# A one-hot product padded from 64 to 128 rows, and the last tile's end moved from GpSimd to VectorE and ScalarE

## The reference, cut to what matters

```python
h = _ln(x, pw_g[pathway_ids], pw_b[pathway_ids])
h = _ln(h, cp_g[compartment_ids], cp_b[compartment_ids])
t = _ln(x, tm_g[time_steps], tm_b[time_steps])
m, n, r = (x + _mlp_ln(state, ...)[:, None, :] for each of three states)
s = _ln(x, ms_g[scale_type], ms_b[scale_type])
cat = concatenate([w[0]*h, w[1]*t, w[2]*m, w[3]*n, w[4]*r, w[5]*s])
x = x + _ln(silu(cat @ int_W1 + int_b1) @ int_W2 + int_b2, int_g, int_be)
```

## Time and profile before

| | |
|---|---|
| time, 3 runs | 1055.29, 1057.88, 1057.75 us; median 1057.75 us |
| profiled execution: its own time, its span | 1056.21 us, 1054.3 us |
| PE busy, share of the span | 996.6 us, 95% |
| DVE, ACT, POOL busy | 664.7 us (63%), 486.1 us (46%), 703.6 us (67%) |
| mean granted clock of TensorE | 0.985 |
| chain that ended last, by engine | PE 76%, DVE 7%, issue 6%, POOL 5%, ACT 3% |

### The profile page before, as it was taken

How to read it: one execution, slowest core, us unless ns; L and a number is a source line. 1 busy time by engine, 2 the same in 40 slices (tenths; PEclk the granted TensorE clock), 3 DMA queues, 4 the chain that set the end, 5 groups by cost and what they waited for, 6 DMA issues and landing times.

```text
span 1054.3 us, 18130 instructions
## 1 busy us (share of the span) xinstructions
PE 996.6 (95%) x6546; PEld 780.5 (74%) x6546; DVE 664.7 (63%) x1210; ACT 486.1 (46%) x763; POOL 703.6 (67%) x635
## 2 busy tenths in 40 slices
PE   6989999999999796999999999999999999999993
PEld 3566777767777475888888887888888888888882
DVE  5677777678768767657557558556556556555441
ACT  2678768775767534334334335324324324323321
POOL 4556665667665348758768768767767767777852
PEclk9989999999999998999999999999999999999997
DMA  9634653544322554232232234233223233132310
GB/s 265 220 118 136 210 212 142 197 167 138 131 88 62 154 178 138 70 104 92 75 115 97 73 111 142 72 95 120 69 92 124 65 101 120 62 108 77 103 42 20
DMA packets 56156, 124.04 MB, mean 118 GB/s; under 512 B 7827, under 2 KB 10005, under 8 KB 55044
## 3 DMA queue, kind: packets, MB, share of 16 engines
q1 hardware_dynamic: 44292, 80.94, 22.9%
q0 software_dynamic: 11776, 41.95, 12.9%
HBM read 104.91 MB, written 17.95 MB: 117 GB/s over the span
## 4 chain that ended last, share of the span: by engine, by line
PE 76%; DVE 7%; issue 6%; POOL 5%; ACT 3%; DMA 1%; SPq 0%; POOLq 0%; DVEq 0%; ACTq 0%
PE ps L597 39%; PE ps_y L604 7%; PE ps_k L669 6%; PE ps_o L604 5%; PE tp L609 5%; PE ps_v L658 2%; PE tp L897 2%; PE ps_s L645 1%; PE ps L976 1%; PE ps_u L690 1%; POOL kb L1669 1%; POOL e L1663 1%; PE ps_z L885 1%; DVE xl L1313 1%; ACT k_diag L993 1%
## 5 line engine op out<-in xcount | busy, mean ns | idle before, releaser
L1715 POOL TENSOR_TENSOR rstd<-var_eps,half 128x1 f32<-128x1 f32 x96 | 54.7, 570 | 118.5 <-DVE var_eps L1510 117.7
L1647 POOL TENSOR_TENSOR om<-om,bc 128x512 f32<-128x512 f32 x32 | 48.1, 1504 | 82.6 <-DVE om L1319 82.6
L1184 ACT ACTIVATE g_out<-ps 128x512 f32<-128x512 f32 x32 | 19.1, 598 | 178.0 <-PE ps L976 178.0
L993 ACT ACTIVATE at_diag<-at 32x512 f32<-32x512 f32 x128 | 80.2, 626 | 7.8 <-DVE at L1293 6.7
L1516 DVE TENSOR_SCALAR shift_n<-mean_var,rstd 128x1 f32<-128x1 f32 x96 | 20.5, 214 | 97.1 <-POOL rstd L1715 95.1
L993 ACT ACTIVATE k_diag<-kt 32x512 f32<-32x512 f32 x128 | 80.1, 625 | 1.1
L1496 DVE TENSOR_TENSOR t_lo<-tp,t_hi 128x512 fp32r<-128x512 f32 x64 | 43.8, 684 | 31.3 <-ACT t_hi L1121 31.3
L1125 ACT ACTIVATE h<-h,shift_n,rstd 128x512 f32<-128x512 f32 x32 | 26.1, 816 | 80.1 <-DVE shift_n L1516 80.1
L1659 POOL TENSOR_SCALAR xb<-xb,bias_o 128x512 f32<-128x512 f32 x32 | 52.2, 1633 | 11.3 <-DMA xb<-in_x_wide 11.2
L1663 POOL TENSOR_TENSOR e<-e,rinv 128x512 f32<-128x512 f32 x32 | 33.6, 1051 | 36.4 <-DVE rinv L1280 36.4
L669 PE MATMUL ps_k<-wk_hi,xh 128*128 128x512 f32 x128 | 55.8, 436 | 0.2 <-DVE xl L1313 0.2
(11 more groups left out here) (286 smaller groups left out, 3240.6 us busy)
## 6 DMA issues: line engine op xcount, KB each, us to landing
raw<-in_dec_w SPq DMA_DIRECT2D x30, 512.0 KB, 6.1
x_in<-in_x_turned SPq DMA_DIRECT2D x32, 256.0 KB, 5.3
xb<-in_x_wide SPq DMA_DIRECT2D x32, 256.0 KB, 4.0
x_dram<-xb SPq DMA_DIRECT2D x32, 256.0 KB, 3.4
xt<-x_dram SPq DMA_DIRECT2D x8, 1024.0 KB, 8.3
out<-o SPq DMA_DIRECT2D x32, 256.0 KB, 2.0
raw<-in_int_W SPq DMA_DIRECT2D x7, 1024.0 KB, 6.6
wk_raw<-in_w_k_t SPq DMA_DIRECT2D x4, 256.0 KB, 6.3
```

The costliest lines, as they stand in the source:

```text
L993: last = nc.scalar.activation(dst[g, :, q, :], src[g, :, :], ACT.Copy)
L1647: nc.gpsimd.tensor_tensor(om[:, :], om[:, :], bc[:, STYLE_O, t // TB, :], ALU.mult).then_inc(mix_step, 1)
L1715: nc.gpsimd.tensor_tensor(rstd[:, k:k + 1], var_eps[:, k:k + 1], half[:, :], ALU.pow).then_inc(norm_step[k], 1)
```

## The change

Three things are edited. `one_hot`, `tab`, `id_rows` and `codes` get 128 rows instead of 64: the added `tab` rows stay zero (they are cleared by the same instruction that clears the tile), the added codes are -1, so the added one-hot rows are zero too. In the last tile's final norm, GpSimd's power is replaced by VectorE's `reciprocal` followed by ScalarE's `Sqrt`. And the last tile's multiplication by `gain` and its residual addition go from GpSimd to VectorE. The other 31 tiles keep their norm and their end.

```diff
# ACT
             def normalize(k, t, dst, src):
-                act.wait_ge(norm_step[k], nth(NORM, "shift", t + 1))
+                act.wait_ge(norm_step[k], nth(NORM, "shift", t + 1) + (k == LN3 and t == T - 1))
...
                 if has(0):
                     high("s", c, tp[1], l3_done, c)
+                if d == T - 1:
+                    act.wait_ge(norm_step[LN3], nth(NORM, "var", T) + 1)
+                    nc.scalar.activation(rstd[:, LN3:LN3 + 1], inverse[:, :], ACT.Sqrt).then_inc(norm_step[LN3], 1)
# DVE
             def shifts(k, t):
-                dve.wait_ge(norm_step[k], nth(NORM, "rstd", t + 1))
+                dve.wait_ge(norm_step[k], nth(NORM, "rstd", t + 1) + (k == LN3 and t == T - 1))
...
                 if has(2):
                     shifts(LN3, f)
+                if f == T - 1:
+                    dve.wait_ge(fn_ready, T)
+                    dve.wait_ge(tables_in, 16 * 3)
+                    nc.vector.tensor_tensor(f2[:, :], f2[:, :], gain[:, :], ALU.mult).then_inc(fg_ready, 1)
+                    dve.wait_ge(fg_ready, T)
+                    dve.wait_ge(stored, 16 * f)
+                    nc.vector.tensor_tensor(o[:, :], f2[:, :], x3s[f % 4][:, :], ALU.add).then_inc(o_ready, 1)
...
                     moments(LN3, d, f2[:, :])
+                if d == T - 1:
+                    dve.wait_ge(norm_step[LN3], nth(NORM, "var", T))
+                    nc.vector.reciprocal(inverse[:, :], var_eps[:, LN3:LN3 + 1]).then_inc(norm_step[LN3], 1)
# POOL
-                if has(2):
+                if has(2) and f < T - 1:     # before the gain product, and again before the residual add
...
-                if has(1):
+                if has(1) and d < T - 1:
                     power(LN3, d)
# tiles and inputs
-        tab = sb("tab", [2 * LOW, F], F32R)
+        tab = sb("tab", [P, F], F32R)
-        M["one_hot"] = sb("one_hot", [2 * LOW, P], F32R)
+        M["one_hot"] = sb("one_hot", [P, P], F32R)
-        M["id_rows"] = sb("id_rows", [2 * LOW, P], I32)
+        M["id_rows"] = sb("id_rows", [P, P], I32)
-    id_rows = np.zeros((T, 2 * LOW, P), np.int32)
-    codes = np.full((2 * LOW, 1), -1.0, np.float32)
+    id_rows = np.zeros((T, P, P), np.int32)
+    codes = np.full((P, 1), -1.0, np.float32)
```

More of the change, by code:

```diff
@@ L214, in body @@
         M[n] for n in ("out_raw", "a_stage", "b2", "gain", "shift", "id_rows", "one_hot", "pid"))
-    stats, mean_var, var_eps, rstd, shift_n = (M[n] for n in ("stats", "mean_var", "var_eps", "rstd", "shift_n"))
+    stats, mean_var, var_eps, inverse, rstd, shift_n = (M[n] for n in ("stats", "mean_var", "var_eps", "inverse", "rstd", "shift_n"))
     hi, lo = M["hi"], M["lo"]
@@ L1742, in refine @@
                     nc.gpsimd.tensor_tensor(ss[:, :], xn[:, :], scal[:, :], ALU.mult).then_inc(s_ready, 1)
-                if has(2):
+                if has(2) and f < T - 1:
                     pool.wait_ge(fg_ready, f + 1)
@@ L1792, in program @@
         tables = {n: sb(n, [P, C, B]) for n in ("scale2", "bias2", "bias1")}
-        tables |= {"codes": sb("codes", [2 * LOW, 1]), "ids": sb("ids", [P, 3, T], I32)}
+        tables |= {"codes": sb("codes", [P, 1]), "ids": sb("ids", [P, 3, T], I32)}
         A, M = {}, {}
@@ L1802, in program @@
             A[n] = sb(n, shape)
-        for n, shape in (("half", [P, 1]), ("stats", [P, 3, 6]), ("mean_var", [P, 3, 2]), ("var_eps", [P, 3]), ("rstd", [P, 3]), ("shift_n", [P, 3])):
+        for n, shape in (("half", [P, 1]), ("stats", [P, 3, 6]), ("mean_var", [P, 3, 2]), ("var_eps", [P, 3]), ("inverse", [P, 1]), ("rstd", [P, 3]), ("shift_n", [P, 3])):
             M[n] = sb(n, shape)
```

## The result

| | before | after |
|---|---|---|
| median of 4 runs | 1056.52 us | 1041.68 us |
| lowest, highest | 1055.04, 1057.88 us | 1038.07, 1044.17 us |
| profiled execution: its own time, its span | 1056.21, 1054.3 us | 1044.17, 1042.4 us |

The ratio is 0.9861 (95% interval 0.983 to 0.9891): 14.8 us faster, where 10.8 had been forecast. The padding and the last tile's three operations did what the prediction says, to within 0.2 us in each stretch. What was missed is a third gain of 5.7 us, in a place that the prediction held fixed: behind the issue of the last store.

The account below looks back on a forecast made before the run. PE was taken to bound the cascade, POOL's loop steps 27 to 30, and one chain the end; 8.9 + 0.4 + 0.2 + 1.3 = 10.8 us off a mean of 1056.8 gave 1046.0 us, range 1043.5 to 1049.0.

Parts of the forecast that it names:

- The padded product: One-hot product on PE: with 128 rows it runs like its neighbours at 0.23 us, saving 0.34 us a tile.
- Rival (1): Rows aren't the cause of the one-hot gaps; only the tail's gain stays, 1055.3 us; chance 0.10.
- 26 tiles keep it: Tiles 0 to 26 without tile 11 keep the 0.34 us each on PE, 8.9 us.
- tile 11: There PE's next matmul waits 0.55 us for DVE's `z`; PE would only wait longer, so the tile gives 0.
- Tiles 27 to 29 give nothing: In steps without a chunk POOL's loop, 16.7 us a round, sets the pace; 1.0 us of padding gain is lost.
- Rival (2): POOL's loop isn't binding, so tiles 27 to 29 keep 1.0 us: 1045.0 us; chance 0.10.
- The wait in front of `ss`: PE's wait before the `ss` transposes grows to about 0.5 us in steps 28 to 30, a sign for tiles 27 to 29.
- rstd of the last tile: Last norm, `var_eps` to `shift_n`: 0.62 us instead of 0.82, 0.2 us saved, table load in ACT's idle hole.
- Rival (3): The Sqrt's table load stands behind its wait and costs 1.3 us: 1047.3 us; chance 0.08.
- Gain and residual: Last tile's two operations on DVE at 0.68 us each: normalize to store 2.26 instead of 3.52 us, 1.26 saved.
- Rival (4): Moved addresses slow most full-tile DVE operations and DVE becomes the bound: some 262 us more, 1308 us; chance 0.03.
- The sum: 8.9 + 0.4 + 0.2 + 1.3 = 10.8 us off the span, 1054.3 to 1043.5; forecast 1046.0 us.

Follow-up runs that it names:

- pad_only: The padding to 128 rows alone against the kernel before, last tile's norm and end unchanged; 1045.04 us, ratio 0.9888 to before.
- pad_96: The kernel after with 96 rows in place of 128 in all the sizes that the change edits; 1040.56 us, ratio 0.9852 to before.
- tail_only: The kernel after with the six sizes back at 64 rows, so only the last tile's edits remain; 1049.84 us, ratio 0.9934 to before.

## Why the prediction was right or wrong

**The padded product** (0.34 us a tile): right. The steps are 0.23, 0.23 and 0.43 us, and pad_only shows them without the tail's edits. The one-hot tile's comparison took 0.29 us, 0.01 more. The forecast reads the same steps at all 32 one-hots; the 0.43 and then 0.49 us of transposes stand behind 30 of them, since no transposes of x3 follow the last two, which the sum treats apart anyway. Rival (1), by which rows are not the cause, is refuted, by pad_96 from the other side too.

**26 tiles keep it**: right. The forecast for the stretch between first and last one-hot is 26 x 0.34 and 0.20 of tile 30, 9.0 us; measured 8.88. From one-hot to one-hot the 26 tiles gave 8.25 us (0.33 each, 0.28 in the steps without a chunk), tile 11 0.36, tiles 27 to 29 0.11 and tile 30 0.15 (0.20 forecast). The 0.36 isn't the padding's: tail_only, with 64 rows, has 19.89 us there, the kernel after 19.86, the kernel before 20.22, and pad_only, with 128 rows, 20.46. Compared with tail_only, the kernel after gains 8.88 us in the 26 tiles and 0.03 in tile 11, just as forecast. Executions thus scatter by some 0.02 us a tile, and by up to 1 us at tile 11, and that the sum came within 0.1 us is luck in part.

**Tiles 27 to 29 give nothing**: right, with 0.11 of 1.0 us. POOL's rounds stayed at 16.6 us or above, PE waits 0.25 and 0.27 us where it did not, and taking the residual addition off POOL gave 1.05 us. Rival (2) is refuted. The wait in front of `ss` was forecast at 0.5 us in steps 28 to 30. From start to start it grew by 0.4 us in steps 29 and 30, which made those steps 16.59 and 16.58 us long against PE's own 16.15, and by less than 0.1 in step 28.

**rstd of the last tile**: right. From `var_eps` to `shift_n` 0.62 us; the `Sqrt` took 0.20. The table load lay in ACT's hole, 1.28 us from 1029.86, 5.9 us ahead of the `Sqrt`. Rival (3), with the load behind the wait, is refuted. The Trainium skill, "ScalarE: Activation LUTs", section Step-by-step: what each stage is for, puts it right before the activation. In order it stands there in this kernel too, but ahead of the activation's wait, 5.9 us early, and costs nothing.

**Gain and residual**: right. 0.69 us each on DVE, the store 2.29 us behind the normalize (2.26 forecast), the tail from last one-hot to store 1.53 us shorter (0.11 + 0.2 + 1.26 = 1.57 forecast). Rival (4), slower DVE operations all through, did not come: DVE has 353.99 us in the cascade, and had 355.24.

**The sum**: this step failed. It took 10.8 us off the span and so left all that lies behind the store's issue as it was, 9.6 us. It became 3.9. The prediction asked which engine is idle during the tail, but not which engine's finish ends the program. The 9.6 us stood in the profile, empty of any busy engine and far over the 2.0 us that the page gives a store to land; what fills them wasn't asked. It is POOL's closing drain, 7.9 us from POOL's last operation, and 1.7 us of semaphore clearing. With POOL done early the end is 3.9 us, 2.0 for the store to land and 1.9 to close. With that term the sum would have been 10.8 + 5.7 = 16.5 us and the forecast 1040.3, 1.4 us under the measured median and inside its runs (1038.07 to 1044.17).

## What to carry to other kernels

Look at what stands between the last store's issue and the end of the span: where that is far more than a store needs to land, find the engine that stops last, and let GpSimd end its last instruction (a wait counts) some 8 us before the last store lands. A matmul of 64 rows among products of 128 cost about 0.3 us each time in gaps around it; zero rows up to 96 or 128 took the gaps away, where the tiles fit. And a gain on the engine that sets the pace is worth only as many steps as no second loop holds: moving work off that loop pays where the engine is full, not where it has a hole.

## What the runs showed of the hardware that was not expected

- GpSimd's closing drain ends 7.9 us after its last operation or wait, in all fifteen executions (record 9.23 to 9.26 us beside a last operation of 1.26 to 1.28 us, 8.52 beside a `power` of 0.55, 8.03 beside a memset of 0.10, 7.91 beside a wait).
- A product of 96 rows stands among 128-row ones without a gap; 64 rows cost 0.34 us, and 2 rows 0.18 us ahead of the product (0.59 against 0.41 with 128).
- The lower clock level can begin while TensorE is at work, amid the 12 matmuls of a product (pitch 0.23 to 0.43 us), and cost 1.4 to 1.6 us in the last tile's out product in five of the fourteen executions profiled beside that of the kernel before.
- DVE's 128x512 operation on two SBUF operands took 0.69 us with POOL idle and 1.51 us (gain) to 1.65 us (residual) with POOL at work; POOL's `tt` went from 1.30 to 1.74 us beside the gain.
